# Second layer of a two-layer graph network on one core: one-hots stationary in four column groups, edge products streamed, inner sums taken after the edge sums

## The chip, the cores and the metric

The kernel runs on one core of one Trainium2 chip. The metric is the device time of one execution in microseconds (us), as the median of several runs. Two times of this kernel can be told apart when they differ by more than about 0.2%.

## The reference

There are 12,500 nodes with 32 features and 400,000 edges, sorted by destination. Two layers run one after the other, each behind a normalisation with a relu. The first adds to each node the weighted features of its sources. The second computes for every edge 256 weights by a small network and multiplies them with the features of the edge's source. `s` are 8 scalars and `v` 8 vectors of three parts per node, and `sh` four numbers per edge:

```python
h = jax.nn.relu(edge_feat @ W1 + b1)                 # 32 -> 64
w = (h @ W2 + b2).reshape(e, 4, 8, 8)                # four 8x8 blocks per edge
m0 = ALPHA * (einsum('ei,eio->eo', s_e * sh0, w_000) + C110 * einsum('eim,em,eio->eo', v_e, sh1, w_110))
m1 = ALPHA * (einsum('ei,em,eio->eom', s_e, sh1, w_011) + einsum('eim,eio->eom', v_e * sh0, w_101))
out = concat(segment_sum(m0, dst), segment_sum(m1, dst)) + self interaction
```

The sum over `i` (8 input channels) and the sum over edges of one destination are both linear, so their order is free.

## The kernel before, in words

Edges are cut into S = 625 supertiles of 640 edges (G = 5 tiles of 128, one edge per partition). Since the edges are sorted, all edges of a supertile fall into a window of 32 nodes. The loop over supertiles is written by hand for each engine (`supertiles`), with a ring of 4 buffers in the second layer (`RING`), and semaphores tie the engines together. Each engine handles its instructions in the order of its own code, so an instruction that waits holds up all behind it.

The first layer runs from the start to about 3190 us of the trace, then sums are folded and normalised, and the second layer runs from about 3280 to 7448 us. Only the second layer is rebuilt by the change. Per supertile n the engines do this in it:

- SyncE loads indices, edge features and `sh`.
- GpSimd issues five indirect DMAs (L359) that gather the source features into `z`. Supertile n waits for `msg1_ready` of n-4, that is, for a free buffer.
- TensorE runs `edge_layer`: the window sums of supertile n-3 (`window_sums`, L602 and L605, into PSUM tile `sc_ps`), the 256 weights of n-1 (`weights`, L596, into one of two PSUM buffers in `w_ps`), among them a small product with selection matrices (`product_sums`, L611), and the hidden layer of n (`hidden`, L589, into `hp_ps`). The profile shows each f32 matmul as two records.
- VectorE runs `products`: `vsh` (L879), `coef` (L881), the one-hots (L743), a reduction (L885), three kinds of products out of PSUM (L887, L892 three times, L898), a reduction (L903), an addition that halves the inner sum (L906), and a last product (L909) that raises `msg1_ready`. Then it adds the finished 32x32 total of an earlier supertile to `acc` (`take_sums`, L754).
- ScalarE does the relu of the hidden layer (L470, L471) and copies the window sums out of PSUM (L475).

In `window_sums` the products (128 columns) are stationary and the one-hots (32 columns) stream. The rest of the sum over `i` is done by `product_sums` on the 32-wide sums.

Of the kernel before, what the change touches and what calls it, by code (L numbers as in the profile page):

```python
# [5 lines left out]
P = 128  # L6
# [4 lines left out]
RING = 4  # L11
R0 = 6
MUL = 8
# [4 lines left out]
HV = (MUL // 2) * 3 * MUL  # L18
# [18 lines left out]
def gnn_two_layers(nc, x, src_t, src_pe, dst_flat, dst_t, ew_t, sh_t, ft, w1_2, b1_2, w2_aug, si_mat, iota,  # L37
                   rows, ident, sel, out):
# [25 lines left out]
    with ExitStack() as ctx:  # L64
# [9 lines left out]
        def sems(name, ring):  # L74
# [15 lines left out]
        sums_ps = sc_ps[:, 0:2 * WIN].rearrange("p (k n) -> p k n", k=2)  # L90
# [28 lines left out]
        sel_sb = sb("sel_sb", [P, 2, D])  # L119
        sums_sb = sb("sums_sb", [P, 2, WIN])  # L120
# [9 lines left out]
        ft_sb = sb("ft_sb", [P, RING, HALF])  # L130
        sh_sb = sb("sh_sb", [P, RING, G, 4])
        hid = sb("hid", [P, 2, SUP])
        coef = sb("coef", [P, G, MUL + D])
# [3 lines left out]
        p101 = sb("p101", [P, G, MUL, 3 * MUL])  # L137
        prod1 = sb("prod1", [P, 2, G, 2 * MUL, MUL])
        prod2 = sb("prod2", [P, 2, G, P])


# [5 lines left out]
        pick = [t[:, 0:GB * P // 2].bitcast(BF16).rearrange("p (b e) -> p b e", b=GB) for t in (  # L147
            prod1[:, 0].rearrange("p g i o -> p (g i o)"), prod1[:, 1].rearrange("p g i o -> p (g i o)"),
            prod2[:, 0].rearrange("p g c -> p (g c)"))]
        group_prod = p101[:].rearrange("p g i c -> p (g i c)")[:, 0:NC * D].rearrange("p (c d) -> p c d", d=D)  # L150
# [11 lines left out]
        cleared, ones_set, pads_set = sem("cleared"), sem("ones_set"), sem("pads_set")  # L162
# [18 lines left out]
        idx1_in, z1_in, sh_in, ft_in = (sems(n, RING) for n in ("idx1_in", "z1_in", "sh_in", "ft_in"))  # L181
        hidpre_ready, hid_ready, wts_ready, wts_used = (
            sem(n) for n in ("hidpre_ready", "hid_ready", "wts_ready", "wts_used"))
        prod_step, msg1_ready, sum1_ready, sum1_copied, total1_ready, acc1_done = (
            sem(n) for n in ("prod_step", "msg1_ready", "sum1_ready", "sum1_copied", "total1_ready", "acc1_done"))
# [35 lines left out]
        wide_partial, wide_copied = sem("wide_partial"), sem("wide_copied")  # L221
# [12 lines left out]
        def _(sp):  # L234
# [5 lines left out]
            for to, of in ((iota_sb, iota), (rows_sb, rows), (id_sb, ident), (sel_sb, sel), (w1_sb, w1_2), (b1_sb, b1_2),  # L240
                           (w2_sb, w2_aug), (si_raw, si_mat)):
                sp.dma_start(to[:], of).then_inc(const_in, 16)
# [75 lines left out]
            def load1(b, r, s):  # L318
                n = b * RING + r
                if s is not None and s < RING:  # L320
# [4 lines left out]
                if s is None or s >= RING:  # L325
                    sp.wait_ge(hidpre_ready, n - RING + 1)
                sp.dma_start(ft_sb[0:2 * D, r, :], ft[n]).then_inc(ft_in[r], 16)
                if s is None or s >= RING:
                    sp.wait_ge(msg1_ready, n - RING + 1)
                sp.dma_start(sh_sb[:, r].rearrange("p g c -> p (g c)"), sh_t[n]).then_inc(sh_in[r], 16)  # L330
            supertiles(sp, RING, load1)
# [7 lines left out]
        def _(pool):  # L339
# [7 lines left out]
            pool.memset(hid[HID:HID + 1], 1.0).then_inc(ones_set, 1)  # L347

# [15 lines left out]
            pool.wait_ge(ones_set, 1)  # L364
# [29 lines left out]
            pool.memset(prod2[:, :, :, HV + 3 * MUL:P], 0.0).then_inc(pads_set, 1)  # L394
            pool.wait_ge(pads_set, 1)
# [3 lines left out]
            supertiles(pool, RING, gathers(RING, h1_dram, idx1_in, z1_in, msg1_ready, G))  # L399
# [4 lines left out]
        def _(act):  # L404
# [3 lines left out]
            nc.scalar.activation(si_sb[:], si_raw[:], ACT.Copy, scale=MUL ** -0.5).then_inc(si_scaled, 1)  # L408
            nc.scalar.activation(iota_ps, iota_sb[:], ACT.Copy).then_inc(consts_ready, 1)
# [64 lines left out]
            def copy_sums():  # L474
                return nc.scalar.activation(sums_sb[:], sums_ps, ACT.Copy)  # L475

            def relu(b, r, s):
                n = b * RING + r

                if s is None or s >= 3:  # L480
                    act.wait_ge(sum1_ready, n - 2)
                    copy_sums().then_inc(sum1_copied, 1)
                if s is not None and s >= S:
                    return
                if s == 0:
                    act.wait_ge(ones_set, 1)
# [3 lines left out]
                relu_halves(r % 2)  # L490
            supertiles(act, RING, relu, lag=3)

            act.wait_ge(acc1_done, S)
            with if_wide(act):
                with act.Fori(0, S) as n:
# [3 lines left out]
                    with act.Fori(0, NWIN) as w:  # L499
                        act.wait_ge(wide_partial, n * NWIN + w + 1)  # L500
                        act.nop(nofuse=True)
                        copy_sums().then_inc(wide_copied, 1)
# [5 lines left out]
        def _(pe):  # L508
# [59 lines left out]
            pe.wait_ge(ones_set, 1)  # L568
# [40 lines left out]
            def product_sums(q):  # L609
                for blk in range(2):  # L610
                    mm = pe.matmul(total1_ps[q], sel_sb[:, blk, :], sums_sb[:, blk, :], start=(blk == 0), stop=(blk == 1))  # L611
                return mm

            def edge_layer(b, r, s):
                n = b * RING + r

                if s is None or s >= 3:
                    v = (r - 3) % RING
                    pe.wait_ge(msg1_ready, n - 2)
                    window_sums(v).then_inc(sum1_ready, 1)  # L620

                def totals():

                    if s is None or s >= 3:
                        pe.wait_ge(sum1_copied, n - 2)
                        if s is None or s >= 4:
                            pe.wait_ge(acc1_done, n - 3)
                        product_sums((r - 3) % 2).then_inc(total1_ready, 1)

                if s is None or 1 <= s <= S:  # L630
                    q = (r - 1) % 2
                    if s == 1:
                        pe.wait_ge(si_added, GR)
                    pe.wait_ge(hid_ready, n)
                    if s is None or s >= 3:
                        pe.wait_ge(wts_used, n - 2)
                    weights(q, totals).then_inc(wts_ready, 1)
                else:
                    totals()
# [6 lines left out]
            supertiles(pe, RING, edge_layer, lag=3)  # L646
# [9 lines left out]
            def wide_sums1(turn):  # L656
                window_sums(0).then_inc(wide_partial, 1)
                pe.wait_ge(wide_copied, turn + 1)
                pe.nop(nofuse=True)
                return product_sums(1)  # L660
# [5 lines left out]
        def _(dve):  # L666
# [80 lines left out]
            def take_sums(n, s, ready, done, total_ps):  # L747

                base = dve.value_load(base_row[0:1, bass.ds(n, 1)], min_val=0, max_val=N - 1)  # L749
                dve.wait_ge(ready, n + 1)  # L750
# [34 lines left out]
            def layer0(b, r, s):  # L785
# [10 lines left out]
                if s is None or s >= 5:  # L796
                    if s == 5:
                        dve.wait_ge(cleared, 1)
                    take_sums(n - 5, None if s is None else s - 5, sum0_ready, acc0_done, total0_ps[(r - 5) % 2])
            supertiles(dve, R0, layer0, lag=5)  # L800

            def wide_supertiles(layer, before, last_add, total_ps):
# [3 lines left out]
                with if_wide(dve):  # L806
# [3 lines left out]
                    with dve.Fori(0, S) as n:  # L810
# [13 lines left out]
                        with dve.Fori(0, NWIN) as w:  # L824
# [3 lines left out]
                                wide_dst[:].unsqueeze(2).to_broadcast([P, G, WIN]), ALU.is_equal).then_inc(hot, 1)  # L828
                            dve.wait_ge(summed, turn + 1)
# [38 lines left out]
            STEPS = 6  # L868

            def products(n, r, q, meanwhile):  # L870

                def step(i):
                    dve.wait_ge(prod_step, n * STEPS + i)

                wts = wts_ps[q]
                s_in, v_in = z[:, r, :, 0:MUL], z[:, r, :, MUL:D]
                sh0, sh1 = sh_sb[:, r, :, 0:1], sh_sb[:, r, :, 1:4]

                nc.vector.tensor_tensor(vsh[:], v_in.rearrange("p g (i m) -> p g i m", m=3),  # L879
                                        sh1.unsqueeze(2).to_broadcast([P, G, MUL, 3]), ALU.mult).then_inc(prod_step, 1)  # L880
                nc.vector.tensor_tensor(coef[:, :, MUL:], z[:, r], sh0.to_broadcast([P, G, D]),  # L881
                                        ALU.mult).then_inc(prod_step, 1)
                meanwhile()
                step(1)
                nc.vector.tensor_reduce(coef[:, :, 0:MUL], vsh[:], AX, ALU.add).then_inc(prod_step, 1)  # L885
                dve.wait_ge(wts_ready, n + 1)
                nc.vector.tensor_tensor(p011[:], wts[:, :, 2 * BLK:3 * BLK].rearrange("p g (i o) -> p g i o", i=MUL),  # L887
# [107 lines left out]
```

## Time and profile before

| | before |
|---|---|
| median of 3 runs | 7470.88 us (7469.18 to 7480.62) |
| the profiled execution's own time | 7511.65 us |
| its span in the trace | 7509.9 us |
| mean granted clock of TensorE | 0.940 |
| second layer, from the trace | 449 supertiles in 3000 us, 6.68 us each |

The busy share of an engine is an average over both layers, so the parts below look at stretches inside the second layer. The profiled execution took 0.5% longer than the median. "Granted clock" is the share of its full 2.4 GHz that TensorE was given, and in the rows it stands at 1.00 or 0.50 (1.2 GHz) or, where a stretch holds both, between.

### The profile page before, as it was taken

The page shows a single profiled execution, that of the slowest core. Times are in us where ns is not written, and L with a number is a line of the kernel's source. Part 1 is how long each engine was busy: PE and PEld are TensorE (multiplying, and loading weights), DVE is VectorE, ACT ScalarE, POOL GpSimd, SP SyncE. Part 2 cuts the span into 40 slices and gives each one's busy share as a digit, 9 for nine tenths or more (in the row PEclk, how much of TensorE's full clock was granted, in tenths as well). Part 3 has the DMA queues.
Part 4 walks back from the last instruction along what each step waited for, and adds up shares of the span by engine and source line. Part 5 has one row for each costly group of instructions (what it writes and reads, how often), then busy time and mean ns, then how long its engine had stood idle before and what let it go on. Part 6 is the DMA issues. An engine that isn't in the chain of part 4 may idle for free.

```text
span 7509.9 us, 156607 instructions
## 1 busy us (share of the span) xinstructions
PE 6878.4 (92%) x43925; PEld 4828.3 (64%) x43925; DVE 5185.1 (69%) x12628; ACT 1611.0 (21%) x5210; POOL 5642.2 (75%) x5686
## 2 busy tenths in 40 slices
PE   5999999999999999969999999999999999999997
PEld 3555555555555555557777777777777777777776
DVE  5666666666666666667777777777777777777775
ACT  1222222222222222231111111111111111111112
POOL 5777777777777777757777777777777777777775
PEclk9999999999999999979989999998989989999997
DMA  3111111111111111111111111111111111111111
GB/s 68 28 27 27 27 27 27 27 27 27 27 27 27 27 27 27 26 26 26 27 26 26 27 26 27 26 26 27 27 26 26 26 26 27 27 26 27 27 27 25
DMA packets 696251, 208.89 MB, mean 28 GB/s; under 512 B 483587, under 2 KB 694099, under 8 KB 695729
## 3 DMA queue, kind: packets, MB, share of 16 engines
q0 software_dynamic: 180000, 92.52, 8.9%
q1 hardware_dynamic: 516232, 116.15, 8.0%
q8 instruction: 7, 0.11, 0.0%
q14 instruction: 12, 0.10, 0.0%
HBM read 202.95 MB, written 5.12 MB: 28 GB/s over the span
## 4 chain that ended last, share of the span: by engine, by line
POOL 58%; issue 28%; PE 6%; DMA 3%; DVE 2%; POOLq 1%; ACT 1%; SPq 0%; DVEq 0%; ACTq 0%
POOL z L359 58%; PE w_ps L521 5%; DMA z<-h_table,idx 2%; DMA feat<-key_table 1%; PE w_ps L531 1%; DVE p L892 0%; POOLq L356 0%; DVE t L903 0%; DMA key_part<-in_src_pe 0%; ACT stage L440 0%; POOLq L192 0%; POOLq L355 0%; ACT z L427 0%; DVE z L782 0%; DVEq L749 0%
## 5 line engine op out<-in xcount | busy, mean ns | idle before, releaser
L359 POOL DMA_INDIRECT z<-h_table,idx x5625 | 5595.9, 995 | 1750.0 <-issue 1680.3
L521 PE MATMUL w_ps<-stage,prod 128*128 128x416 bf16 x15000 | 2744.3, 339 | 198.8 <-DVE z L782 113.0
L521 PEld LDWEIGHTS w_ps<-stage,prod 128*128 128x128 bf16 x15000 | 1418.7, 98 | 1313.0 <-issue 164.9
L596 PE MATMUL w_ps<-w_sb,hid 128*128 128x256 f32 x6250 | 1949.1, 450 | 2.5 <-ACT hid L471 2.5
L596 PEld LDWEIGHTS w_ps<-w_sb,hid 128*128 128x128 f32 x6250 | 1260.7, 219 | 184.2 <-issue 1.8
L427 ACT ACTIVATE z<-z,ew_sb 128x32 f32<-128x32 f32 x3125 | 732.8, 309 | 2394.2 <-DMA z<-h_table,idx 2240.7
L762 DVE TENSOR_TENSOR prod<-hp_ps,feat 128x1024 bf16<-128x1024 f32 x625 | 765.1, 1224 | 599.1 <-DMA feat<-key_table 586.9
L602 PEld LDWEIGHTS sc_ps<-onehot,prod 128*128 128x128 f32 x6250 | 774.8, 194 | 585.9 <-DVE prod L909 549.1
L602 PE MATMUL sc_ps<-onehot,prod 128*128 128x32 f32 x6250 | 800.9, 276 | 349.7 <-DVE prod L909 348.8
L605 PE MATMUL sc_ps<-onehot,prod 128*128 128x32 f32 x6250 | 870.0, 289 | 0.0
L879 DVE TENSOR_TENSOR vsh<-z,sh_sb 128x120 f32<-128x120 f32 x625 | 180.7, 289 | 993.4 <-DMA z<-h_table,idx 993.1
L605 PEld LDWEIGHTS sc_ps<-onehot,prod 128*128 128x128 f32 x6250 | 816.3, 207 | 0.0
L892 DVE TENSOR_TENSOR p<-w_ps,coef 128x320 f32<-128x320 f32 x1875 | 795.3, 478 | 0.0
L470 ACT ACTIVATE hid<-hp_ps,b_sb 64x320 f32<-64x320 f32 x625 | 326.5, 522 | 2174.7 <-PE hp_ps L589 2174.7
L754 DVE TENSOR_TENSOR acc<-acc,w_ps 32x32 f32 x1250 | 220.3, 176 | 558.6 <-PE w_ps L531 370.4
L782 DVE TENSOR_REDUCE z<-p 128x32 f32<-128x416 f32 x625 | 538.5, 862 | 21.3
L898 DVE TENSOR_TENSOR prod<-w_ps,coef 128x640 f32<-128x640 f32 x625 | 506.3, 810 | 0.0
L903 DVE TENSOR_REDUCE t<-p 128x40 f32<-128x320 f32 x625 | 446.1, 714 | 0.0
L589 PE MATMUL hp_ps<-ft_sb,w_sb 128*128 128x320 f32 x1250 | 443.3, 436 | 0.0
L906 DVE TENSOR_TENSOR prod<-p 128x480 f32<-128x480 f32 x625 | 402.9, 645 | 0.0
L475 ACT ACTIVATE sums_sb<-sc_ps 128x64 f32<-128x64 f32 x625 | 140.2, 224 | 1208.2 <-PE sc_ps L605 1207.2
L531 PEld LDWEIGHTS w_ps<-onehot,z 128*32 128x32 f32 x6250 | 244.7, 112 | 228.8 <-issue 204.9
(63 smaller groups left out, 3350.9 us busy)
## 6 DMA issues: line engine op xcount, KB each, us to landing
z<-h_table,idx POOLq DMA_INDIRECT x5625
ft_sb<-in_ft SPq DMA_DIRECT2D x625, 80.0 KB
feat<-key_table SPq DMA_DIRECT2D x625, 64.0 KB
idx<-in_src_t SPq DMA_DIRECT2D x1250, 2.5 KB
ew_sb<-in_ew_t SPq DMA_DIRECT2D x625, 2.5 KB
sh_sb<-in_sh_t SPq DMA_DIRECT2D x625, 10.0 KB
h_table<-big SPq DMA_DIRECT2D x10, 312.5 KB
x_sb<-in_x SPq DMA_DIRECT2D x1, 1562.5 KB
```

Of the source, the lines that this page charges most:

```text
L359: pool.indirect_dma_start(z[:, r, u, :], None, rows, bass.IndirectOffsetOnAxis(ap=idx[:, r, u:u + 1], axis=0)).then_inc(z_in[r], 16)
L427: last = nc.scalar.activation(z[:, r, u, :], z[:, r, u, :], ACT.Copy, scale=ew_sb[:, r, u:u + 1])
L521: mm = pe.matmul(fold_ps[:, k, 0:NC * D], pick[k][:, blk, :], parts[:, t, :, blk, :], start=(blk == 0 and t == 0), stop=(blk == GB - 1 and ...
L589: return pe.matmul(hp_ps[:, 0:HALF], w1_sb[:], ft_sb[:, r, :], start=True, stop=True)
L596: mm = pe.matmul(wts_ps[q][:, u, :], hid[:, q, u * P:(u + 1) * P], w2_sb[:], start=True, stop=True)
L602: pe.matmul(sums_ps[:, 0, :], prod1[:, r % 2, u].rearrange("p i o -> p (i o)"), onehot[:, r, u, :], start=(u == 0), stop=(u == G - 1))
L605: mm = pe.matmul(sums_ps[:, 1, :], prod2[:, r % 2, u, :], onehot[:, r, u, :], start=(u == 0), stop=(u == G - 1))
L762: nc.vector.tensor_tensor(pick[k], rows_ps.unsqueeze(2).to_broadcast([P, GB, P]), key[:, k].unsqueeze(1).to_broadcast([P, GB, P]), ALU.is_ ...
L782: nc.vector.tensor_reduce(z[:, r, GT, :], group_prod.rearrange("p c d -> p d c"), AX, ALU.add).then_inc(selected, 1)
L892: last = nc.vector.tensor_tensor(p101[:, :, :, m * MUL:(m + 1) * MUL], wts[:, :, 3 * BLK:].rearrange("p g (i o) -> p g i o", i=MUL), coef_ ...
L898: nc.vector.tensor_tensor(prod1[:, q], wts[:, :, 0:2 * BLK].rearrange("p g (i o) -> p g i o", o=MUL), coef[:, :, 0:2 * MUL].unsqueeze(3).t ...
L903: nc.vector.tensor_reduce(t011[:], p011[:].rearrange("p g i o -> p g o i"), AX, ALU.add).then_inc(prod_step, 1)
```

## The change

The second layer is rebuilt, and the first is only renumbered (its scratch tiles lie elsewhere).

- `window_sums`: the one-hots (128x32) are now stationary and the products stream as 320 columns. Tiles u = 0 to 3 go to the four column groups of TensorE (output partitions 32u to 32u+31), the fifth tile is split in four quarters of 80 columns, one for each group, and five products of 24 columns (`tail`) are added. The result is a 128x320 sum in one PSUM buffer, `sums_ps`.
- `reduce_sums`: VectorE sums over `i` on these 320 columns (two reductions out of PSUM), and TensorE folds the four groups with one matmul (`fold_sums`), in place of ScalarE's copy and two matmuls.
- The sums of supertile n-3 have one PSUM buffer. TensorE waits for `sum1_reduced` before it writes the next.
- The one-hots are made on ScalarE (five `Abs` with `rel_sb` as bias, one `Relu`, L497 and L508) and loaded as weights, and the product of `z` with `sh0` is also done there, five instructions a supertile (`scale_rows`, L480).
- VectorE: three products of 320 become one of 960, and the addition L906, the product `coef` (L881) and the one-hots (L743) go away.
- The ring has 6 buffers in place of 4 (`R1`). Input columns and `w2` are permuted to fit.

The core of the diff:

```diff
-            def window_sums(r):
+            def window_sums(r, v):
+                quarter = MUL * PC // 4
...
+                for u in range(G - 1):
+                    pe.matmul(sums_ps[part(u), :], onehot[:, r, u, :], columns(u), start=True, stop=False)
                 for u in range(G):
-                    pe.matmul(sums_ps[:, 0, :], prod1[:, r % 2, u].rearrange("p i o -> p (i o)"),
-                              onehot[:, r, u, :], start=(u == 0), stop=(u == G - 1))
-                for u in range(G):
-                    mm = pe.matmul(sums_ps[:, 1, :], prod2[:, r % 2, u, :], onehot[:, r, u, :],
-                                   start=(u == 0), stop=(u == G - 1))
+                    pe.matmul(sums_i[part(u % 4), 0, 2 * MUL:PC], onehot[:, r, u, :], tail[:, v, u, :],
+                              start=False, stop=False)
+                for k in range(4):
+                    cols = slice(k * quarter, (k + 1) * quarter)
+                    mm = pe.matmul(sums_ps[part(k), cols], onehot[:, r, G - 1, :], columns(G - 1)[:, cols],
+                                   start=False, stop=True)
                 return mm
...
+            def fold_sums(k, q):
+                return pe.matmul(total1_ps[q], reduced_sb[:, k].rearrange("p o c -> p (o c)"), stacked_sb[:],
+                                 start=True, stop=True)
...
                 if s is None or s < S:
                     pe.wait_ge(ft_in[r], (b + 1) * 16)
                     if s is None or s >= 1:
                         pe.wait_ge(hid_ready, n)
                     hidden(r).then_inc(hidpre_ready, 1)
...
+                def total():
+                    if s is None or s >= 6:
+                        pe.wait_ge(sum1_reduced, n - 5)
+                        return fold_sums(r % 2, q)
+                if s is None or 1 <= s <= S:
+                    weights(q, total).then_inc(wts_ready, 1)
...
+                if s is None or 3 <= s <= S + 2:
+                    v = (r - 3) % R1
+                    pe.wait_ge(msg1_ready, n - 2)
+                    pe.wait_ge(hot1_ready, n - 2)
+                    if s is None or s >= 4:
+                        pe.wait_ge(sum1_reduced, n - 3)
+                    window_sums(v, v % 3).then_inc(sum1_ready, 1)
```

On VectorE:

```diff
+            def reduce_sums(k):
+
+                nc.vector.tensor_reduce(reduced_sb[:, k, :, 0],
+                                        sums_i[:, :, 0:2 * MUL].rearrange("p i (b o) -> p o i b", b=2),
+                                        mybir.AxisListType.XY, ALU.add)
+                return nc.vector.tensor_reduce(reduced_sb[:, k, :, 1:4].rearrange("p o m -> p m o"),
+                                               sums_i[:, :, 2 * MUL:PC].rearrange("p i (m o) -> p m o i", m=3),
+                                               AX, ALU.add)
...
+                def reduce():
+                    if s is None or 3 <= s <= S + 2:
+                        dve.wait_ge(sum1_ready, n - 2)
+                        reduce_sums((r - 3) % 2).then_inc(sum1_reduced, 1)
```

The order of instructions on TensorE, one step of the second layer's loop. Before, the step begins with the window sums of n-3 (`sc_ps`), goes on to the weights of n-1 (`w_ps`) and ends with the hidden layer of n (`hp_ps`):

```order
L602 MATMUL sc_ps<-onehot,prod 128x32 [waits msg1_ready]
L602 MATMUL sc_ps<-onehot,prod 128x32 x4
L605 MATMUL sc_ps<-onehot,prod 128x32 x5
L634 REGISTER_ALU
L596 MATMUL w_ps<-w_sb,hid 128x256 [waits wts_used,hid_ready]
L596 MATMUL w_ps<-w_sb,hid 128x256 x3
L611 MATMUL w_ps<-sums_sb,sel_sb 32x32 [waits acc1_done,sum1_copied]
L611 MATMUL w_ps<-sums_sb,sel_sb 32x32
L596 MATMUL w_ps<-w_sb,hid 128x256
L589 MATMUL hp_ps<-ft_sb,w_sb 128x320 [waits hid_ready,ft_in1]
```

After, the same step begins with the hidden layer of n, then come the weights of n-1, and the window sums of n-3 stand last:

```order
L608 MATMUL hp_ps<-ft_sb,w_sb 128x320 [waits hid_ready]
L615 MATMUL w_ps<-w_sb,hid 128x256 [waits wts_used,hid_ready]
L615 MATMUL w_ps<-w_sb,hid 128x256 x3
L639 MATMUL w_ps<-stacked_sb,reduced_sb 32x32 [waits sum1_reduced]
L615 MATMUL w_ps<-w_sb,hid 128x256
L628 MATMUL sc_ps<-prod,onehot 32x320 [waits sum1_reduced,hot1_ready,msg1_ready]
L628 MATMUL sc_ps<-prod,onehot 32x320 x3
L630 MATMUL sc_ps<-tail,onehot 32x24 x5
L634 MATMUL sc_ps<-prod,onehot 32x80 x4
```

The window sums have moved behind the weights, and their first matmul has two more semaphores to wait for, `sum1_reduced` among them.

The order on VectorE in one step n of the same loop, after the change (`wts_ready` is TensorE's weights of n, `sum1_ready` the window sums of n-3; the second of the two L907/L910 reductions raises `sum1_reduced`):

```order
L926 TENSOR_TENSOR vsh<-z,sh_sb 128x120 [waits sh_in1,z1_in1]
L929 TENSOR_REDUCE coef<-vsh 128x40 [waits prod_step]
L932 TENSOR_TENSOR p<-w_ps,z 128x320 [waits wts_ready]
L786 TENSOR_TENSOR acc<-acc,w_ps 32x32
L936 TENSOR_TENSOR prod<-w_ps,coef 128x40x24 [waits coef_ready]
L940 TENSOR_TENSOR prod<-w_ps,coef 128x40x16 [waits prod_step]
...
L945 TENSOR_REDUCE t<-p 128x40 [waits prod_step]
L907 TENSOR_REDUCE reduced_sb<-sc_ps 128x8 [waits sum1_ready]
L910 TENSOR_REDUCE reduced_sb<-sc_ps 128x3x8
L949 TENSOR_TENSOR tail<-t,sh_sb 128x120 [waits prod_step]
```

Before, VectorE's step had no reduction out of `sc_ps`, and nothing on TensorE waited for a reduction. Now the two stand behind the step's products and ahead of its last one.

## Rows read from the trace of the kernel before

**Rows 1.** Windows: stretch, length, busy of PE, PEld, DVE, ACT, POOL, clock, DMA.

```profile
4000.00:7000.00 3000.00, 2749.75 (x16171) 2244.35 (x16171) 2174.03 (x5840) 570.62 (x1347) 2315.53 (x2246) 0.91 0.16 27
```

**Rows 2.** Who waited for whom, 4000 to 7000 us: total, times, longest.

```profile
DVE vsh L879 <- DMA z<-h_table,idx: 707.7, 446, 2.0
PE sc_ps L602 <- DVE prod L909: 249.7, 269, 1.4
```

**Rows 3.** Groups by shape, 4000 to 7000 us: busy us, mean ns, idle before.

```profile
L359 POOL DMA_INDIRECT z<-h_table,idx x2246 | 2315.9, 1031 | 684.8 <-issue 667.7 <-DVE prod L909 17.1
L892 DVE TENSOR_TENSOR p<-w_ps,coef 128x320 f32<-128x320 f32 x1350 | 572.7, 478 | 0.0
L903 DVE TENSOR_REDUCE t<-p 128x40 f32<-128x320 f32 x449 | 320.5, 714 | 0.0
L885 DVE TENSOR_REDUCE coef<-vsh 128x40 f32<-128x120 f32 x449 | 120.5, 268 | 0.0
```

**Rows 4.** First layer, 1000 to 3000 us, by shape.

```profile
L359 POOL DMA_INDIRECT z<-h_table,idx x1600 | 1513.5, 946 | 488.0 <-issue 484.1 <-PE w_ps L531 4.0
L427 ACT ACTIVATE z<-z,ew_sb 128x32 f32<-128x32 f32 x2000 | 467.6, 309 | 1533.8 <-DMA z<-h_table,idx 1533.8
```

**Rows 5.** Timeline of one supertile at full clock: start, length, instruction, count.

```profile
5001.03 1.97 PE L596 MATMUL w_ps<-w_sb,hid 128*128 128x256 f32 x8
5001.69 0.48 DVE L887 TENSOR_TENSOR p<-w_ps,z 128x320 f32<-128x320 f32 x1
5002.09 1.27 DVE L892 TENSOR_TENSOR p<-w_ps,coef 128x320 f32<-128x320 f32 x3
5003.28 0.81 DVE L898 TENSOR_TENSOR prod<-w_ps,coef 128x640 f32<-128x640 f32 x1
5003.71 0.70 PE L589 MATMUL hp_ps<-ft_sb,w_sb 128*128 128x320 f32 x2
5004.01 0.71 DVE L903 TENSOR_REDUCE t<-p 128x40 f32<-128x320 f32 x1
5004.64 0.65 DVE L906 TENSOR_TENSOR prod<-p 128x480 f32<-128x480 f32 x1
5004.74 1.37 POOL L359 DMA_INDIRECT z<-h_table,idx  x1 [0.30 <-issue]
5005.54 1.30 PE L602 MATMUL sc_ps<-onehot,prod 128*128 128x32 f32 x10 [1.12 <-DVE prod L909]
5005.66 0.18 DVE L754 TENSOR_TENSOR acc<-acc,w_ps 32x32 f32 x1 [0.18 <-issue]
5007.79 1.97 PE L596 MATMUL w_ps<-w_sb,hid 128*128 128x256 f32 x8
```

**Rows 6.** Timeline of the first layer: ten records into one column group.

```profile
3122.35 0.50 PE L531 MATMUL w_ps<-onehot,z 128*32 128x32 f32 x10
```

**Rows 7.** Windows on TensorE: stretch, length, busy (records), granted clock, DMA.

```profile
5038.25:5039.10 0.85, 0.04 (x1) 1.00 0.17 19
5039.10:5039.95 0.85, 0.85 (x8) 0.92 0.00 0
5039.95:5040.80 0.85, 0.85 (x6) 0.50 0.24 31
...
5045.90:5046.75 0.85, 0.85 (x7) 0.56 0.00 0
```

**Rows 8.** Timeline after TensorE had waited 3.34 us, and at half clock.

```profile
3287.78 1.45 PE L602 MATMUL sc_ps<-onehot,prod 128*128 128x32 f32 x10 [3.34 <-DVE prod L909]
3291.17 3.76 PE L596 MATMUL w_ps<-w_sb,hid 128*128 128x256 f32 x8
```

**Rows 9.** Windows around that wait.

```profile
3285.00:3290.00 5.00, 2.23 (x15) 0.88 0.15 29
3290.00:3295.00 5.00, 5.00 (x18) 0.50 0.19 33
```

More of the change, by code:

```diff
@@ L10 @@
 WIN = 32
-RING = 4
 R0 = 6
+R1 = 6
 MUL = 8
@@ L318, in load1 @@
             def load1(b, r, s):
-                n = b * RING + r
-                if s is not None and s < RING:
+                n = b * R1 + r
+                if s is not None and s < R1:
                     sp.wait_ge(z0_in[r], uses(r) * 16 * GT)
@@ L472, in relu_halves, with scale_rows @@
                                      bias=b1_sb[HID:P]).then_inc(hid_ready, 1)
-            def copy_sums():
-                return nc.scalar.activation(sums_sb[:], sums_ps, ACT.Copy)
-            def relu(b, r, s):
[L478 to L484, printed above, removed]
+            def scale_rows(n, r, q):
+                for u in range(G):
+                    last = nc.scalar.activation(coef[:, q, u, :, 1:5], z[:, r, u, :].rearrange("p (i c) -> p i c", c=4),
+                                                ACT.Copy, scale=sh_sb[:, r, u, 0:1])
+                last.then_inc(coef_ready, 1)
+            def relu(b, r, s):
+                n = b * R1 + r
+                q = r % 2
                 if s == 0:
-                    act.wait_ge(ones_set, 1)
+                    act.wait_ge(ones_set, 2)
                 act.wait_ge(hidpre_ready, n + 1)
@@ L489, in relu @@
                     act.wait_ge(wts_ready, n - 1)
-                relu_halves(r % 2)
-            supertiles(act, RING, relu, lag=3)
+                relu_halves(q)
+                if s is None or s >= 1:
+                    act.wait_ge(hot1_ready, n)
+                for u in range(G):
+                    last = nc.scalar.activation(near[:, u, :], iota_sb[:], ACT.Abs, scale=-1.0,
+                                                bias=rel_sb[:, bass.ds(n * G + u, 1)])
+                last.then_inc(near_ready, 1)
+                act.wait_ge(z1_in[r], (b + 1) * 16 * G)
+                act.wait_ge(sh_in[r], (b + 1) * 16)
+                if s is None or s >= 2:
+                    act.wait_ge(wts_used, n - 1)
+                scale_rows(n, r, q)
+                act.wait_ge(near_ready, n + 1)
+                nc.scalar.activation(onehot[:, r], near[:], ACT.Relu, scale=-1.0, bias=one_sb[:]).then_inc(hot1_ready, 1)
+            supertiles(act, R1, relu)
             act.wait_ge(acc1_done, S)
@@ L609, in product_sums, with columns, part @@
[L609 to L612, printed above, removed]
+            def window_sums(r, v):
+                quarter = MUL * PC // 4
+                def columns(u):
+                    return prod[:, v, u].rearrange("p i c -> p (i c)")
+                def part(k):
+                    return slice(k * WIN, (k + 1) * WIN)
+                for u in range(G - 1):
+                    pe.matmul(sums_ps[part(u), :], onehot[:, r, u, :], columns(u), start=True, stop=False)
+                for u in range(G):
+                    pe.matmul(sums_i[part(u % 4), 0, 2 * MUL:PC], onehot[:, r, u, :], tail[:, v, u, :],
[4 more added lines that the diff above has]
+                                   start=False, stop=True)
+                return mm
@@ L630, in edge_layer @@
[L630 to L639, printed above, removed]
+                n = b * R1 + r
+                q = (r - 1) % 2
                 if s is None or s < S:
@@ L872, in step, with products @@
+            def products(n, r, q, v, ready, take, reduce):
                 def step(i):
                     dve.wait_ge(prod_step, n * STEPS + i)
[L875 to L880, printed above, removed]
@@ L898, in products @@
-                nc.vector.tensor_tensor(
-                    prod1[:, q], wts[:, :, 0:2 * BLK].rearrange("p g (i o) -> p g i o", o=MUL),
-                    coef[:, :, 0:2 * MUL].unsqueeze(3).to_broadcast([P, G, 2 * MUL, MUL]),
-                    ALU.mult).then_inc(wts_used, 1)
-                step(4)
+                nc.vector.tensor_reduce(cf[:, :, 0], vsh[:].rearrange("p g i m -> p (g i) m"), AX, ALU.add
+                                        ).then_inc(prod_step, 1)
+                dve.wait_ge(wts_ready, ready)
```

215 lines of the change are left out of this document (115 added, 100 removed).

## The prediction

> **What bounds it now.** The change touches only the second layer, so I read a stretch inside it. [rows 1] give the busy time of each engine over 3000 us: TensorE 2750, VectorE 2174, ScalarE 571. TensorE looks like the bound, but this column counts busy at half clock too. The waits say more. VectorE waits 708 us for the gather of `z`, and TensorE waits 250 us for VectorE's last product [rows 2]. So TensorE waits for VectorE, and VectorE waits for GpSimd. GpSimd itself is full [rows 3]: 2246 gathers are busy for 2316 us and stand idle 685 us before them, 668 of it "issue", which is the engine's own 0.30 us between two gathers. Only 17 us is waiting for a free buffer. Five gathers take 5 x (1.031 + 0.305) = 6.68 us, and that is the period of a supertile: 3000/449 = 6.68. GpSimd sets the pace of the second layer, and the others fit under it.
>
> The gathers are slowed by something: in the first layer one takes 946 ns [rows 4], here 1031 on average, and the one that begins at 5004.74 takes 1.37 us, while VectorE runs L906 with both operands in SBUF [rows 5].
>
> **What the change does, part by part.**
>
> *GpSimd.* L906, the one-hots and `coef` leave VectorE, and they are instructions whose inputs are both in SBUF. If these were all that stretched the gathers, five would take 5 x (0.946 + 0.305) = 6.26 us. If nothing changes, 6.68. I take 6.35, since `vsh` and the last product stay. This alone would be a gain of 0.33 x 625 = 206 us. It counts only if nothing else needs more than 6.35 us.
>
> *ScalarE.* It gets five `Abs` and five scalings of 128x32, priced by the nearest row at 309 ns each [rows 4], so 3.1 us, a relu of the one-hots at some 0.4, and its two old relus of 0.52. Less the copy of 0.22, that makes about 4.5 us a supertile. All of it is for supertile n, whose sums come three steps later, so it hides below any period over 5 us. If its cover went it would cost nothing here, for it is not in the loop below.
>
> *The new loop of waits.* This is the part that decides. The order shows TensorE's step n+1 as hidden n+1, weights n, window sums of n-2, and the window sums wait for `sum1_reduced` of n-3. The reduction of n-3 stands in VectorE's step n, behind the products of n. These wait for `wts_ready` of n, so for the weights that TensorE did just ahead in that same step n+1. Then TensorE can't go on to hidden n+2 and weights n+1 before the window sums, since it works in order. And VectorE's step n+1 needs weights n+1. So each supertile goes once round: weights ready, VectorE's products and reduction, window sums, hidden, weights ready. Nothing overlaps but VectorE's ends (last product, `vsh`, first reduction, some 0.8 us), which run under TensorE. A second buffer for the weights doesn't help, nor does the ring of 6. Before, the window sums waited only for products of a supertile whose weights had been made a full step earlier, so the two engines ran side by side.
>
> The period is then a sum, D + W, of VectorE's part and TensorE's.
>
> D, from `wts_ready` to `sum1_reduced`, by the distance from start to start in [rows 5]:
> - handover: 0.10, and 0.05 on the way back;
> - `p011` 0.40 (5001.69 to 5002.09);
> - `take_sums` 0.18 and a little of its idle 0.18: 0.25;
> - one product of 960 columns: 320 cost 478 ns [rows 3] and 640 cost 0.81, so 1.04 ns a column and 0.145 fixed, makes 1.14, of which 0.08 overlaps the next: 1.06;
> - the product of 640: 0.73 (5003.28 to 5004.01);
> - the reduction over 320: 0.63 (5004.01 to 5004.64);
> - two new reductions of 128 and 192 columns out of PSUM with strides. No row shows such. The dense L885 takes 268 ns for 120, the strided L903 714 for 320 [rows 3]. With 1.04 ns a column and 0.15 fixed they are 0.28 + 0.35; by the line from L885 to L903, 2.23 ns a column, 0.29 + 0.43. PSUM and the longer stride could make it 1.0. I take 0.78 together.
>
> D = 0.15 + 0.40 + 0.25 + 1.06 + 0.73 + 0.63 + 0.78 = 4.0 us, with bounds 3.7 and 4.4.
>
> W, at full clock. Weights and hidden with the small product lasted from 5001.03 to 5004.41, 3.38 us [rows 5]; the fold is one matmul instead of two: 3.3. The new window sums have no row, and depend on how far the column groups run at once. L596 took 1.97 us for 8 records of 256 columns, so 0.246 each [rows 5]. That gives some 0.30 for 320 columns, and 8 records of these, 10 of 24 columns at 0.05 each (ten records of 32 columns in one group took 0.50 [rows 6]) and 8 of 80 columns at about 0.08. If nothing overlaps: 2.4 + 0.5 + 0.6 = 3.5. If the four groups overlap fully: a quarter, 0.9. If a group's second record must follow its first before the next group may start, the big ones take five lengths instead of eight: 1.5 + 0.4 + 0.3 = 2.2. I take 2.2, the middle. The old ones took 2.25 (5005.54 to 5007.79), so nothing is gained there.
>
> The Trainium skill's page "TensorE: Matmul & The Clock Gate", section on packing small matmuls, has a measured 2.38 times for three column tiles, and says that matmuls start and end strictly in order. By its factor the big part would shrink from 2.4 to about 1.0 and the period by 0.5 us against mine; by its order rule it would be my 2.2. No row here shows two column groups at work.
>
> So at full clock the period is 4.0 + 3.3 + 2.2 = 9.5 us.
>
> *The clock.* TensorE would stand idle for 4.0 us in each period. In the trace, after a wait of 3.34 us [rows 8] the clock is 0.88 in the 5 us around, then 0.50 [rows 9]. Even a gap of 1.1 us brings at times such a fall: at 5039.1 from 1.00 to 0.50, until 5045.9, so 6.8 us long [rows 7]. Such dips make the 0.91 of [rows 1]. At half clock the eight records of L596 take 3.76 us in place of 1.97 [rows 5, 8]. I expect one dip in each period, which begins near the end of the gap. About 6.3 us of it fall on TensorE's work, which gets 6.3 x 1.97/3.76 = 3.3 us of full-clock work done. It costs 3.0 us. The period becomes 12.5 us, the mean clock of the layer about 0.7.
>
> The same page, section on the clock gate, says that a stretch of idleness takes the clock to half and that activity gives it back; the trace agrees, with the dips above. It would give the same 12.5.
>
> **The sum.** 7511.65 + 625 x (12.5 - 6.68) = 7512 + 3637 = 11149 us for a profiled execution. The profiled one was 41 us above the median of before, so I say 11110 us. First layer, folds and ends stay.
>
> **The rivals.**
> - *The loop binds, but the clock keeps up.* Period 9.5, with well-overlapping groups 8.2: 7471 + 625 x 2.8 = 9230, down to 8420. For it: between dips the old kernel has gaps of 1.1 us and keeps 1.00 for several supertiles. Against it: the gap here is 4.0, and 3.34 was enough. 0.14.
> - *The column groups don't overlap at all, and the dips come.* W is 6.8, and the period 4.0 + 6.8 + 3.0 = 13.8: 11920. 0.12.
> - *GpSimd stays the bound and is relieved.* If the ends of the two engines' parts overlapped so that the loop took under 6.68 us, the layer would go by the gathers at 6.35: 7471 - 206 = 7265. The point from which it decides is D + W = 6.68, and D alone with the weights and the hidden layer is 7.3 with window sums of no length. It needs reductions that don't wait for the same step's weights, against the order shown. 0.02.
> - *No change.* The loop would have to land just on 6.68: 0.01.
>
> **How the numbers follow.** The likeliest case has 0.71: D from 3.7 to 4.4, window sums from 0.9 to 2.8, a dip that costs 2 to 3.5 us. That gives periods from 10.8 to 13.5. The range for 8 in 10 reaches a little into both neighbours: period 10.4 to 13.9, so 9800 to 12000 us. Less than 0.2% (15 us) can't be told from no change here; slower by more has 0.97, within it 0.01, faster 0.02.
>
> **What would show it.** VectorE's longest wait is no longer for the gather but for the weights (`wts_ready`), GpSimd waits for a free buffer, and TensorE's first window sum waits some 4 us for `reduced_sb` of VectorE in every step. The granted clock of the layer stands near 0.7. The gathers without these waits are near 0.96 us each. I am wrong if VectorE still waits for `z`, if TensorE's wait is under 3 us, or if the clock stays above 0.9.

## The result, and the profile after

| | before | after |
|---|---|---|
| median | 7470.03 us (4 runs) | 9722.62 us (9721.84 to 9723.57, 4 runs) |
| ratio | | 1.301, 95% interval 1.299 to 1.304 |
| mean granted clock | 0.940 | 0.774 |
| period of a supertile in the second layer | 6.68 us | 10.24 us |

The kernel became 30% slower. The first layer kept its time, and 625 x (10.24 - 6.68) = 2225 us of the 2253 us lie in the second layer.

The waits of the changed kernel from 5000 to 9000 us (who waited for whom, total, times, longest):

```profile
ACT hid L474 <- PE hp_ps L608: 2577.7, 390, 6.7
DVE p L932 <- PE w_ps L615: 2234.8, 391, 5.8
POOL z L363 <- DVE tail L949: 1676.9, 391, 4.3
PE sc_ps L628 <- DVE reduced_sb L910: 1421.0, 391, 3.7
```

These answer to [rows 2]. VectorE no longer waits for the gather, but 5.7 us in each supertile for the weights of TensorE (L615). TensorE waits 3.6 us in each for the second reduction, and GpSimd for a free buffer. No engine is full. The groups of the same stretch (busy us, mean ns, idle before), beside [rows 3]:

```profile
L363 POOL DMA_INDIRECT z<-h_table,idx x1953 | 1848.4, 946 | 2152.9 <-DVE tail L949 1676.9 <-issue 475.7 <-DMA idx<-in_src_t 0.3
L936 DVE TENSOR_TENSOR prod<-w_ps,coef 128x960 f32<-128x960 f32 x391 | 445.3, 1139 | 0.0
L910 DVE TENSOR_REDUCE reduced_sb<-sc_ps 128x24 f32<-128x192 f32 x391 | 131.7, 337 | 0.0
L907 DVE TENSOR_REDUCE reduced_sb<-sc_ps 128x8 f32<-128x128 f32 x391 | 105.5, 270 | 0.0
```

The gathers are back at 946 ns. One turn round the loop, in the timeline (start, length, instruction):

```profile
6003.23 0.70 PE L615 MATMUL w_ps<-w_sb,hid 128*128 128x256 f32 x2
6003.97 0.49 DVE L932 TENSOR_TENSOR p<-w_ps,z 128x320 f32<-128x320 f32 x1 [5.81 <-PE w_ps L615]
6004.47 1.14 DVE L936 TENSOR_TENSOR prod<-w_ps,coef 128x960 f32<-128x960 f32 x1
6005.54 0.80 DVE L940 TENSOR_TENSOR prod<-w_ps,coef 128x640 f32<-128x640 f32 x1
6006.27 0.70 DVE L945 TENSOR_REDUCE t<-p 128x40 f32<-128x320 f32 x1
6007.10 0.34 DVE L910 TENSOR_REDUCE reduced_sb<-sc_ps 128x24 f32<-128x192 f32 x1
6007.58 1.29 PE L628 MATMUL sc_ps<-prod,onehot 128*32 128x320 f32 x8 [3.65 <-DVE reduced_sb L910]
6009.24 1.44 PE L608 MATMUL hp_ps<-ft_sb,w_sb 128*128 128x320 f32 x2
6010.46 2.90 PE L615 MATMUL w_ps<-w_sb,hid 128*128 128x256 f32 x8
6013.47 0.70 PE L615 MATMUL w_ps<-w_sb,hid 128*128 128x256 f32 x2
6014.21 0.49 DVE L932 TENSOR_TENSOR p<-w_ps,z 128x320 f32<-128x320 f32 x1 [5.81 <-PE w_ps L615]
```

The weights end at 6003.93, VectorE's products and reductions fill 3.65 us, then TensorE does window sums, hidden layer and weights, and the next `L932` starts 10.24 us after the last. The brackets show the loop: VectorE's wait (5.81 us) ends with TensorE's weights, and TensorE's wait (3.65 us) ends with VectorE's second reduction.

TensorE's clock over this turn (stretch, length, busy, granted clock):

```profile
6005.50:6006.00 0.50, 0.00 (x0) 0.68 0.00 0
6006.00:6006.50 0.50, 0.00 (x0) 0.50 0.00 0
...
6012.00:6012.50 0.50, 0.50 (x2) 0.50 0.00 0
6012.50:6013.00 0.50, 0.50 (x4) 1.00 0.24 33
```

A share of 0.68 over the first half microsecond puts the clock's fall at 6005.7, 1.9 us before TensorE's wait ends. It comes back at 6012.5, 6.8 us later. Such a stretch at 1.2 GHz is called a dip here. All but the last 1.7 us of TensorE's work of this turn lies in it. In the trace's clock records the 293 turns from 4000 to 7000 us have 293 dips, each 6.8 us long.

### The profile page after: what moved, and what is told of

It reads as the page before. It is cut to its first block, busy times and chain, and to the rows that moved or that the text cites. A ratio compares the mean times of both kernels' runs of the same rounds, so it can differ in the third digit from the quotient of the medians.

```text
span 9721.6 us, 166257 instructions
## 1 busy us (share of the span) xinstructions
PE 7174.7 (74%) x46425; PEld 4313.6 (44%) x46425; DVE 4794.5 (49%) x10753; ACT 3061.9 (31%) x11461; POOL 5373.5 (55%) x5686
## 4 chain that ended last, share of the span: by engine, by line
PE 48%; POOL 17%; issue 16%; DVE 14%; DMA 2%; DVEq 1%; ACT 1%; POOLq 0%; SPq 0%; ACTq 0%
PE w_ps L615 21%; POOL z L363 17%; PE hp_ps L608 9%; PE sc_ps L628 8%; DVE prod L940 5%; PE w_ps L540 5%; DVE t L945 4%; PE sc_ps L634 2%; DVE reduced_sb L910 2%; PE w_ps L639 1%; DVE acc L786 1%; DMA z<-h_table,idx 1%; DMA feat<-key_table 1%; PE sc_ps L630 1%; DVE reduced_sb L907 1%
## 5 line engine op out<-in xcount | busy, mean ns | idle before, releaser
L628 PE MATMUL sc_ps<-prod,onehot 128*32 128x320 f32 x5000 | 808.9, 737 | 2262.2 <-DVE reduced_sb L910 2262.2
L615 PE MATMUL w_ps<-w_sb,hid 128*128 128x256 f32 x6250 | 2258.4, 510 | 0.0
L932 DVE TENSOR_TENSOR p<-w_ps,z 128x320 f32<-128x320 f32 x625 | 307.1, 491 | 3555.1 <-PE w_ps L615 3555.1
L615 PEld LDWEIGHTS w_ps<-w_sb,hid 128*128 128x128 f32 x6250 | 1691.3, 278 | 544.6 <-issue 244.0
L608 PE MATMUL hp_ps<-ft_sb,w_sb 128*128 128x320 f32 x1250 | 895.8, 820 | 9.9 <-ACT hid L475 9.9
L497 ACT ACTIVATE near<-iota_sb,rel_sb 128x32 f32<-128x32 f32 x3125 | 730.6, 309 | 16.4
L480 ACT ACTIVATE coef<-z,sh_sb 128x32 f32<-128x32 f32 x3125 | 720.5, 306 | 15.1 <-DMA z<-h_table,idx 15.1
L936 DVE TENSOR_TENSOR prod<-w_ps,coef 128x960 f32<-128x960 f32 x625 | 711.9, 1139 | 0.4 <-ACT coef L480 0.4
L814 DVE TENSOR_REDUCE z<-prod 128x32 f32<-128x416 f32 x625 | 538.0, 861 | 21.3
L630 PEld LDWEIGHTS sc_ps<-tail,onehot 128*32 128x32 f32 x6250 | 315.5, 173 | 388.5 <-issue 388.2
L945 DVE TENSOR_REDUCE t<-p 128x40 f32<-128x320 f32 x625 | 437.9, 701 | 0.0
L810 DVE TENSOR_TENSOR prod<-w_ps,group_hot 128x416 f32<-128x416 f32 x625 | 370.0, 592 | 21.9
L608 PEld LDWEIGHTS hp_ps<-ft_sb,w_sb 128*128 128x128 f32 x1250 | 313.3, 312 | 150.6 <-issue 150.3
```

Of the source, the lines that this page charges most:

```text
L480: last = nc.scalar.activation(coef[:, q, u, :, 1:5], z[:, r, u, :].rearrange("p (i c) -> p i c", c=4), ACT.Copy, scale=sh_sb[:, r, u, 0:1])
L497: last = nc.scalar.activation(near[:, u, :], iota_sb[:], ACT.Abs, scale=-1.0, bias=rel_sb[:, bass.ds(n * G + u, 1)])
L608: return pe.matmul(hp_ps[:, 0:HALF], w1_sb[:], ft_sb[:, r, :], start=True, stop=True)
L615: mm = pe.matmul(wts_ps[q][:, u, :], hid[:, q, u * P:(u + 1) * P], w2_sb[:], start=True, stop=True)
L628: pe.matmul(sums_ps[part(u), :], onehot[:, r, u, :], columns(u), start=True, stop=False)
L936: nc.vector.tensor_tensor(pr[:, :, 2 * MUL:PC].rearrange("p e (m o) -> p e m o", m=3), wts[:, :, 3 * MUL:4 * MUL].unsqueeze(2).to_broadcas ...
```

## The experiments

The kernel before took 7480 to 7499 us beside these runs, but for one that is named below. Periods are 3000 us divided by the supertiles from 4000 to 7000 us.

**1. The reductions first.** Only the place of `reduce()` changes.

```diff
                 dve.wait_ge(wts_ready, ready)
+                reduce()
...
-                reduce()
                 step(4)
```

> VectorE's two reductions of the window sums are moved ahead of the step's products, right behind the wait for the weights. Nothing is left out. Theory of the loop: the way round is then handover 0.1 + reductions 0.6 + TensorE's 4.2 at full clock = 4.9 us, less than the five gathers need (5 x (0.947 + 0.305) = 6.26 us), so GpSimd sets the pace again: period 6.3 us, or up to 6.9 if the clock still dips, and 7240 to 7600 us in all. Rival, that TensorE's own work in the new form is the length (window sums, half clock), whoever waits: the period stays above 9 us, over 8900 us.

Measured: 7258.18 us (5 runs), ratio to the kernel before 0.970 (0.969 to 0.972). The period is 6.27 us. Waits from 4000 to 7000 us:

```profile
ACT coef L480 <- DMA z<-h_table,idx: 1198.9, 478, 2.8
DVE vsh L926 <- DMA z<-h_table,idx: 859.8, 478, 2.3
POOL z L363 <- issue: 728.6, 2391, 0.3
```

VectorE waits for the gather again, and GpSimd for nothing but itself. So the theory holds and its rival falls. Two instructions of VectorE in another place are worth 2464 us, and the whole kernel is then 3% faster than before. It is the fastest version of this study.

**2. Work in the gap.** Six idle matmuls between the weights and the window sums, in the main loop.

```diff
+                    if s is None:
+                        pe.wait_ge(wts_used, n - 1)
+                        for _ in range(6):
+                            pe.matmul(wts_ps[1 - q][:, 0, :], id_sb[:], w2_sb[:], start=True, stop=True)
                     pe.wait_ge(msg1_ready, n - 2)
```

> Six matmuls of 128x256 without use are put between the weights and the window sums, into the weight buffer that is free just then, so that TensorE is busy in about 3 us of its 3.65 us wait. They add work, and the result is unchanged. Theory: the loop of waits is 3.65 + 4.2 = 7.9 us at full clock, and the rest of the 10.24 us is the clock's dip: the granted clock goes to about 1.0 and the period to 7.9 to 8.1 us, 8250 to 8400 us in all. Rival, that TensorE's part is as long by itself and the dip only falls where it waits: 10.2 us or more, since 3 us of work are added, 9700 us or more.

Measured: 8256 us (1 run), mean clock 0.990, period 7.87 us, with 3 us of work added to each supertile:

```profile
4000.00:7000.00 3000.00, 2601.36 (x19811) 1947.72 (x19811) 1607.18 (x3810) 1368.77 (x4953) 1802.42 (x1906) 1.00 0.13 22
```

The timeline shows one turn at full clock:

```profile
6000.81 0.49 DVE L936 TENSOR_TENSOR p<-w_ps,z 128x320 f32<-128x320 f32 x1 [3.45 <-PE w_ps L615]
6004.43 0.74 PE L628 MATMUL sc_ps<-prod,onehot 128*32 128x320 f32 x8 [1.06 <-DVE reduced_sb L914]
6005.32 0.81 PE L608 MATMUL hp_ps<-ft_sb,w_sb 128*128 128x320 f32 x2
6008.70 0.49 DVE L936 TENSOR_TENSOR p<-w_ps,z 128x320 f32<-128x320 f32 x1 [3.46 <-PE w_ps L615]
```

From the weights' end (6000.78) to the window sums 3.65 us, these sums 0.89, hidden layer and weights 3.35: together 7.89. So of the 10.24 us, 7.9 are the loop and 2.35 the clock.

**3. One column group.** The output partitions of the window sums are all those of group 0, and the counts of matmuls are unchanged.

> All matmuls of the window sums but those of the first supertile go to the first column group, so the other three groups hold stale sums and the second layer's result is not the reference's; counts and shapes of instructions are the same. Theory that the four groups work at once: eight records of 320 columns, now 1.29 us at half clock, take some 4 us, and the period grows by 2.5 to 3.5 us to about 13 us, 11400 us in all. Rival, that the groups ran one after the other and the records are simply short: the period stays at 10.2 us, 9720 us.

Measured: 10788 us (1 run), period 11.95 us. Two rows of one turn:

```profile
6014.45 4.45 PE L629 MATMUL sc_ps<-prod,onehot 128*32 128x320 f32 x8 [3.65 <-DVE reduced_sb L911]
6020.58 1.89 PE L615 MATMUL w_ps<-w_sb,hid 128*128 128x256 f32 x8
```

At half clock the eight big records take 4.45 us where they took 1.29, so the four groups work at once. The period grew by 1.7 us only, less than the 2.5 to 3.5 expected: the dip passes over the longer window sums, and hidden layer and weights then run at full clock (1.89 us for the eight records of L615, in place of 2.90).

**4 and 5. The reductions a little forward, a little back.** First ahead of the reduction L945 (0.63 us earlier), then behind the step's last product.

> The two reductions are moved only one instruction forward, ahead of the reduction over 320 columns (0.63 us from start to start). Nothing is left out. If the period is the plain sum round the loop: 10.24 - 0.63 = 9.6 us, 9330 us in all. If the clock's dip takes part of it back (less idle time, the dip lies elsewhere): between 9.6 and 10.24 us, up to 9720 us. If the loop is not what binds: 10.24 us and 9720 us with TensorE still waiting 3.65 us.

> The changed kernel with the two reductions moved one instruction back, behind the step's last product (0.26 us). Nothing is left out. Moving them 0.63 us forward left the period at 10.24 us. If the clock's dip sets the period, as that suggests, TensorE's wait grows from 3.65 to 3.9 us, the period stays 10.24 us and the time 9720 us. If the way round adds up plainly and the run before was limited otherwise: 10.50 us, 9880 us.

Measured: 9720.30 and 9721.52 us (1 run each), against 9722.62. The wait did change. Of the first, then of the second:

```profile
6005.05 1.29 PE L628 MATMUL sc_ps<-prod,onehot 128*32 128x320 f32 x8 [3.02 <-DVE reduced_sb L910]
6015.30 1.30 PE L628 MATMUL sc_ps<-prod,onehot 128*32 128x320 f32 x8 [3.02 <-DVE reduced_sb L910]
```

```profile
6005.87 1.30 PE L628 MATMUL sc_ps<-prod,onehot 128*32 128x320 f32 x8 [3.97 <-DVE reduced_sb L910]
6016.37 0.75 PE L628 MATMUL sc_ps<-prod,onehot 128*32 128x320 f32 x8 [3.98 <-DVE reduced_sb L910]
```

TensorE waits 3.02 us in the one and 3.97 in the other, and the mean period is 10.24 us in both. With the 4.24 us of TensorE's work at full clock (experiment 2) the loop is 7.26 us in the one and 8.21 in the other, so the dips cost 3.0 and 2.0 us, where they cost 2.35 with the wait of 3.65. Where the dip lies tells why. With the short wait (experiment 4):

```profile
6004.00:6004.50 0.50, 0.00 (x0) 0.00 (x0) 0.50 (x2) 0.00 (x0) 0.00 (x0) 0.92 0.00 0
6007.94 3.53 PE L615 MATMUL w_ps<-w_sb,hid 128*128 128x256 f32 x8
```

The clock falls at 6004.4, 0.6 us before the wait ends and not 1.9, and again for 6.8 us. So more of the dip lies on work: the eight records of L615 take 3.53 us where they took 2.90, and the 0.63 us saved are spent again. With the long wait 114 of the 293 dips last only 3.4 us. The plain sum with a fixed price for the dip is wrong over this stretch. The loop looks locked to the clock's falls and rises, which is what the equal periods suggest; nothing here shows it by itself.

**6. Forward by 1.36 us.** The reductions stand between the products of 960 and of 640.

> The reductions stand behind the product of 960 columns and ahead of that of 640, 0.73 + 0.63 = 1.36 us earlier than in the changed kernel. Nothing is left out. The way round at full clock is then 3.65 - 1.36 + 4.2 = 6.5 us, just over the 6.26 us of the gathers. If TensorE's idle 2.3 us in 6.5 still brings a dip in each period, about 2.4 us are added: 8.9 us or a step of the clock's rhythm near it, 8900 us in all. If the dips come seldom: 6.5 to 7 us, 7400 to 7700 us.

Measured: 7774 us (1 run), period 7.11 us, mean clock in the stretch 0.90. TensorE waits 2.29 us in a turn:

```profile
6006.52 1.30 PE L628 MATMUL sc_ps<-prod,onehot 128*32 128x320 f32 x8 [2.29 <-DVE reduced_sb L910]
6024.19 0.75 PE L628 MATMUL sc_ps<-prod,onehot 128*32 128x320 f32 x8 [2.29 <-DVE reduced_sb L910]
```

At full clock a turn is 2.29 + 0.89 + 3.35 = 6.5 us; some turns are that (6021.90 to 6028.42 between the weights' ends), others have a dip, which costs up to 3 us. Against experiment 4 the time fell by 1946 us. The shorter wait alone is 625 x 0.73 = 456 us of it; the rest is dips that no longer come. The clock records have 133 in 422 turns, 99 of them 3.4 us long, where experiment 4 had one of 6.8 us in every turn.

**7. The kernel before without its addition.** L906 is left out in the main loop.

> The kernel before, with the addition that halves the inner sum (128x480, both inputs in SBUF) left out in all but the first and the last supertiles of the second layer, so its result is stale there and the output is not the reference's. Theory that VectorE instructions with both inputs in SBUF hold up the gather under way: the gather of 1.37 us falls to about 0.95, the mean from 1.031 to about 0.95 to 0.97, the period from 6.68 to 6.26 to 6.35 us, 7210 to 7270 us in all. Rival, that the gathers were slow for another reason (the other such instructions, or the buffers): the period stays above 6.6 us, over 7420 us.

Measured: 7263.89 us (4 runs), ratio 0.971 (0.970 to 0.973). The gathers, from 4000 to 7000 us:

```profile
L359 POOL DMA_INDIRECT z<-h_table,idx x2387 | 2273.3, 952 | 727.5 <-issue 727.5
```

The 1031 ns of [rows 3] become 952. A gain as large as that of experiment 1 over the old kernel is there in the old kernel itself, with one instruction of 0.65 us gone.

**8. Reductions first, one column group.**

> The reductions first, as in the first experiment, and all window sums but those of the first supertile in one column group, so the other groups hold stale sums and the second layer's result is not the reference's. The loop is then handover and reductions 0.7 + TensorE's 3.3 + window sums of some 3.2 us in place of 0.9 = 7.2 us, above the 6.26 us of the gathers: 7850 us in all, and more if the clock dips. If column groups are worth nothing once the loop is short: 6.3 us and 7260 us as before.

Measured: 7842.59 us (1 run), period 7.21 us. The timeline (TensorE's rows):

```profile
6004.49 2.31 PE L629 MATMUL sc_ps<-prod,onehot 128*32 128x320 f32 x8 [0.83 <-DVE reduced_sb L911]
6007.60 0.81 PE L608 MATMUL hp_ps<-ft_sb,w_sb 128*128 128x320 f32 x2
```

In one group the window sums take 3.11 us, in four 0.89: 3.5 times less. With one group the way round is 0.83 + 3.11 + 3.35 = 7.3 us, which is above the 6.26 us of the gathers and sets the pace.

**9 and 10. The addition with one input.** The kernel before, and the same sum as a reduction over pairs.

```diff
-                nc.vector.tensor_tensor(prod2[:, q, :, 0:HV].rearrange("p g (i c) -> p g i c", i=MUL // 2),
-                                        p101[:, :, 0:MUL // 2], p101[:, :, MUL // 2:], ALU.add)
+                nc.vector.tensor_reduce(prod2[:, q, :, 0:HV],
+                                        p101[:].rearrange("p g (h i) c -> p g (i c) h", h=2), AX, ALU.add)
```

> The kernel before, with its addition of the two halves (two inputs in SBUF, 0.65 us) written as one reduction over pairs, which reads a single input of 960 elements and computes the same. Nothing is left out. By the price of strided reductions in SBUF (714 ns for 320 elements, 268 for 120) it takes 1.2 to 1.9 us, and VectorE has 5.5 to 6.1 us of work in a supertile. If the two inputs hold up the gather: gathers at 0.95 us and a period of 6.3 us, up to 6.6 if VectorE is the next limit, 7240 to 7430 us in all. If any VectorE instruction on SBUF at that place would do it: the gather under it grows by at least as much as now, and the period is 6.7 us or more, 7470 us or more.

> The same kernel once more, since in the last run the kernel before itself took 10327 us in place of 7480 and waits of up to 12 us stood in both that have no releaser in the program. Nothing is left out. If two SBUF inputs are what holds up a gather: gathers at 0.95 us, a period of 6.3 us or, with VectorE near its limit (the reduction took 1157 ns in the last trace, so 5.4 us of work), up to 6.5, 7240 to 7370 us in all. If it is not that: a period of 6.7 us or more, 7470 us or more.

In the first of the two runs the kernel before took 10327 us and this one 10416, and the trace of this one has waits of 10 us and more (up to 32.7) that nothing in the program releases, so it tells nothing of the addition. In the second it took 7277.68 us (4 runs), ratio 0.971 (0.969 to 0.972). Groups from 4000 to 7000 us:

```profile
L359 POOL DMA_INDIRECT z<-h_table,idx x2382 | 2275.4, 955 | 726.2 <-issue 722.5 <-DVE prod L909 3.4 <-DMA idx<-in_src_t 0.3
L906 DVE TENSOR_REDUCE prod<-p 128x480 f32<-128x960 f32 x477 | 550.7, 1155 | 0.0
```

And the timeline of the place where the gather took 1.37 us in [rows 5]:

```profile
5001.40 1.16 DVE L906 TENSOR_REDUCE prod<-p 128x480 f32<-128x960 f32 x1
5001.49 0.95 POOL L359 DMA_INDIRECT z<-h_table,idx  x1 [0.31 <-issue]
```

VectorE's instruction is 0.51 us longer, lies over the gather from its start to its end, and doesn't hold it up. The kernel gains 3% by a slower instruction, and none of the rebuild is needed for it.

So work on VectorE does not by itself slow a gather. Is it the kind of instruction, an elementwise one in place of a reduction? The trace of the kernel before answers that: from 4000 to 7000 us 448 gathers start under L898, which is elementwise too but reads one input from PSUM, and none takes more than 0.96 us. What is left is the second input in SBUF. The same trace also shows when it counts. Beside the gather of 5004.74, which starts 0.10 us into L906, stand these:

```profile
5000.83 0.28 DVE L879 TENSOR_TENSOR vsh<-z,sh_sb 128x120 f32<-128x120 f32 x1 [1.74 <-DMA z<-h_table,idx]
5000.90 1.03 POOL L359 DMA_INDIRECT z<-h_table,idx  x1 [0.31 <-issue]
5001.03 0.32 DVE L881 TENSOR_TENSOR coef<-z,sh_sb 128x160 f32<-128x160 f32 x1
5001.26 0.32 DVE L743 TENSOR_TENSOR onehot<-iota_sb,rel_sb 128x160 f32<-128x160 f32 x1
5002.24 0.95 POOL L359 DMA_INDIRECT z<-h_table,idx  x1 [0.30 <-issue]
```

L879, L881 and L743 all have two inputs in SBUF and follow one another for 0.75 us, yet the gather of 5000.90 loses only 0.08 us. When it starts, L879 has 0.21 us left to run; when the gather of 5004.74 starts, L906 has 0.55 left, and it loses 0.42. Both lose what is left of the instruction under way less 0.13 us; in all, 379 gathers of this stretch start under L906 and lose 0.41 us or more, at most 0.63. And the 70 gathers of this stretch that start ahead of L906 and still run when it begins take 0.95 us. So the loss falls on a gather that starts while such an instruction runs, and a gather already under way goes on unharmed. That is read from one trace; no run moved the gather's start on purpose.

## Why the prediction was wrong

The direction and the mechanism were right, the size was not: 11110 us were forecast, with a range from 9800, and 9723 came.

- *What bounded it before* was right: GpSimd, five gathers of 1.031 + 0.305 us. That L906 stretched the gather was right too, shown by experiments 7 and 10. Forecast was 6.35 us for relieved gathers, measured 6.27 (experiment 1).
- *The loop of waits* was right, shown by experiment 1: cutting it takes the whole loss away, and the waits of after name each of its hands. ScalarE's added work costs nothing, as said: in experiment 1 it waits 1199 us in 3000 for the gather.
- *D* was put at 4.0 us and measured 3.65 between the end of the weights and the start of the window sums. The two reductions took 270 and 337 ns, 0.54 us from the first one's start at 6006.90 to the second one's end, in place of 0.78; they cost the dense price, though they read PSUM with strides of 40 columns. `p011` and `take_sums` took 0.50 us (6003.97 to 6004.47) in place of 0.65.
- *W, the window sums*, is the first step that failed: "If a group's second record must follow its first before the next group may start [...] I take 2.2, the middle". It was 0.89 at full clock, the lower bound. The four groups overlap almost fully (experiments 3 and 8): in the trace of experiment 2 four of the eight big records start within 0.02 us of one another and the other four 0.27 us later, so a group's second record does not hold back the next group. That is 1.3 us of the 2.26 by which the period was too long, 12.5 against 10.24. The Trainium skill, page "TensorE: Matmul & The Clock Gate", section on packing small matmuls, gives 2.38 times for three column tiles; here four gave 3.5 times (3.11 to 0.89 us), and my reading of its rule of order as a limit on the groups was mine, not the page's, and wrong.
- *The clock's dip* was mis-sized: "It costs 3.0 us". It came in each period, as forecast, and lasted 6.8 us, as said, but it began 1.9 us before the gap's end instead of near it, so 4.9 us of it fell on work instead of 6.3. It cost 2.35 us. Nor is it a fixed term of the sum: it cost 3.0 us with the wait of experiment 4 and 2.0 with that of experiment 5. The mean clock of the layer was 0.67, forecast 0.7.
- Together: 1.31 + 0.35 + 0.65 us, less 0.05 (hidden layer and weights took 3.35 us, not 3.3), make the 2.26, nearly all to the same side. The sum of them, not one, put the time below the range: with the window sums right and all else as forecast the period would have been 11.2 us, inside it.
- *The range* was drawn narrower than its own terms. The prediction gives "periods from 10.8 to 13.5" for them, but their lower ends add up to 3.7 + 3.3 + 0.9 + 2.0 = 9.9 us and their upper ends to 4.4 + 3.3 + 2.8 + 3.5 = 14.0. The 10.24 us lie between these, and the range began at 10.4.
- *The rivals.* The clock did not keep up, the groups did overlap, and GpSimd was the bound only once experiment 1 had cut the loop.

Left open: why the mean period is the same 10.24 us for waits of 3.02, 3.65 and 3.97 us is told here only as what the traces show; no run varied TensorE's work in fine steps at one wait. A second PSUM buffer for the window sums, so that TensorE need not wait for the latest reduction, would be another way out of the loop; it was not tried.

## What to carry to other kernels

When two engines each wait for the other's result of the same turn, their times add, and buffers elsewhere don't help: this kernel has a ring of 6 and two weight buffers and waited all the same. Write down for each wait which turn's instruction raises it and what stands ahead of that instruction on its engine: two reductions behind the products instead of in front of them cost 34% here (9723 us against 7258). And look for what stretches the busiest engine's own instructions before rebuilding the work around it.

## What the runs showed of the hardware

- A gather (indirect DMA issued by GpSimd) takes 0.95 us and took 1.37 us when it started under a VectorE addition of 480 f32 columns with both inputs in SBUF. Under a one-input reduction of 1155 ns it took 0.95. The Trainium skill, page "SBUF — State Buffer", section "Who interferes with whom", says that a VectorE instruction with two SBUF inputs contends with a GpSimd instruction that reads SBUF. The trace agrees if the gather counts as one, with its indices in SBUF; that it is this read which waits is not shown. The same section infers that such an instruction doesn't hold up the making of descriptors, and for the indirect gather the measurement says otherwise.
- The gather lost what was left of that VectorE instruction at its start, less 0.13 us (0.55 left, 0.42 lost; 0.21 left, 0.08 lost), and nothing if it had started first (70 gathers of the kernel before).
- Four column groups with 32 stationary columns and 320 f32 columns streamed work at once: eight records in 0.74 us at 2.4 GHz against 2.31 us in one group, and 1.29 against 4.45 us at 1.2 GHz.
- A loop that leaves TensorE idle for 3.02, 3.65 or 3.97 us in each turn had one dip of the clock in each turn and the same mean period of 10.24 us. With 2.29 us there were 133 dips in 422 turns. Adding 3 us of useless matmuls in the wait of 3.65 us took all dips away and made each turn 2.4 us shorter.
